# A fused attention and quantized-FFN block on one core: 16-bit split products for q, latent, k and v, new work lists, aligned loops, and q's and k's high halves weighed from PSUM

## The reference, cut to what matters

```python
xn = layernorm(x)
q = xn @ Wq; lat = (xn @ Wk + xn @ Wv) @ W_down_kv          # latent: 64 wide
k, v = lat @ W_up_k, lat @ W_up_v
scores = clip(q_h @ k_h.T / 16) * exp(-1e-4 * |i - j|)      # 16 heads of 16
y = concat(softmax(scores) @ v_h) @ Wo
x1 = x + layernorm(y)
xh = layernorm(x1) @ H
z = quantize_4bit_per_token(xh) @ ternary(weight).T
out = x1 + layernorm(z)
```

## Time and profile before

| | |
|---|---|
| Median of 3 runs | 1436.37 us |
| All runs | 1433.69, 1436.37, 1437.82 us |
| Span of the profiled execution (the page gives no other time of it) | 1433.2 us |
| Granted clock of PE, mean | 0.983 |
| PE, DVE, ACT, POOL busy | 94%, 82%, 77%, 58% |
| Chain that ended last: PE, DVE, issue, ACT, DMA | 76%, 8%, 5%, 4%, 3% |
| Batches in the steady loop | 26 of 32 |

### The profile page before, as it was taken

How to read it: one execution, slowest core, us unless ns; L and a number is a source line. 1 busy time by engine, 2 the same in 40 slices (tenths; PEclk the granted TensorE clock), 3 DMA queues, 4 the chain that set the end, 5 groups by cost and what they waited for, 6 DMA issues and landing times.

```text
span 1433.2 us, 35971 instructions
## 1 busy us (share of the span) xinstructions
PE 1349.5 (94%) x12330; PEld 600.5 (42%) x12330; DVE 1179.9 (82%) x2739; ACT 1098.2 (77%) x1125; POOL 834.7 (58%) x1238
## 2 busy tenths in 40 slices
PE   5889999999999999999999999999999999999863
PEld 3334444444444444444444444444444444443332
DVE  7567888888888888888888888888888888888655
ACT  1878787888888788878878887887888787787831
POOL 4223655666565666556557655656765655675446
PEclk9999999999999999999999999999999999999986
DMA  6455456556555645656564565655556555555420
GB/s 194 154 167 170 154 172 202 155 164 206 164 182 173 197 156 166 206 157 190 173 190 157 173 201 157 193 175 187 156 177 194 163 185 184 176 156 175 128 77 31
DMA packets 174557, 241.45 MB, mean 168 GB/s; under 512 B 28336, under 2 KB 145200, under 8 KB 174512
## 3 DMA queue, kind: packets, MB, share of 16 engines
q1 hardware_dynamic: 140176, 206.78, 46.5%
q10 hardware_dynamic: 34336, 34.08, 7.7%
HBM read 154.80 MB, written 69.21 MB: 156 GB/s over the span
## 4 chain that ended last, share of the span: by engine, by line
PE 76%; DVE 8%; issue 5%; ACT 4%; DMA 3%; SPq 2%; POOL 2%; DVEq 0%; ACTq 0%; POOLq 0%
PE heads_ps L720 27%; PE scores_ps L707 16%; PE misc_ps L603 8%; PE misc_ps L635 7%; PE misc_ps L660 4%; PE misc_ps L614 3%; PE misc_ps L587 3%; ACT probs L909 2%; DVE x_hl L1204 2%; PE misc_ps L595 2%; PE misc_ps L678 2%; DVE diagonal L1253 2%; DVE weighted L1161 2%; PE misc_ps L625 2%; PE misc_ps L669 1%
## 5 line engine op out<-in xcount | busy, mean ns | idle before, releaser
L909 ACT ACTIVATE probs<-scores_ps 128x1024 f32<-128x1024 f32 x768 | 759.8, 1026 | 248.0 <-PE scores_ps L707 247.9
L720 PE MATMUL heads_ps<-probs,v_sb 128*32 128x512 f32 x4096 | 525.4, 603 | 3.6 <-DVE heads L1150 1.9
L1253 DVE TENSOR_TENSOR diagonal<-scores_ps,comp 128x1024 f32<-128x1024 f32 x256 | 312.2, 1219 | 70.1 <-PE scores_ps L707 70.1
L707 PE MATMUL scores_ps<-q_rep,k_rep 64*128 64x128 f16 (+2 forms) x5120 | 324.6, 251 | 16.0 <-DVE diagonal L1253 9.2
L707 PEld LDWEIGHTS scores_ps<-q_rep,k_rep 64*128 64x128 f16 x5120 | 165.6, 94 | 348.7 <-DVE diagonal L1253 149.5
L916 ACT ACTIVATE probs<-diagonal 128x2048 f32<-128x2048 f32 x128 | 246.0, 1922 | 0.0
L996 POOL TENSOR_TENSOR ln_neg_mean<-zero,ln_moments 128x4 f32<-128x4 f32 (+1 forms) x131 | 34.6, 264 | 356.5 <-DVE ln_moments L1115 356.3
L1161 DVE SCALAR_TENSOR_TENSOR weighted<-misc_ps,edges 128x384 f32<-128x384 f32 x256 | 129.4, 547 | 64.3 <-PE misc_ps L603 33.8
L720 PEld LDWEIGHTS heads_ps<-probs,v_sb 128*32 128x32 f32 x4096 | 91.5, 108 | 171.7 <-issue 169.8
L1038 POOL TENSOR_TENSOR q_hl<-weighted,q_hl 128x768 f16<-128x768 f32 x64 | 105.5, 1648 | 77.5 <-DVE q_hl L1168 77.5
L1043 POOL TENSOR_TENSOR heads_c<-heads_c,den_spread 128x1024 f32<-128x1024 f32 (+1 forms) x33 | 75.7, 2296 | 111.0 <-DMA den_spread<-den_scratch 111.0
(11 more groups left out here) (132 smaller groups left out, 1511.5 us busy)
## 6 DMA issues: line engine op xcount, KB each, us to landing
q_rep<-q_scratch SPq DMA_DIRECT2D x128, 384.0 KB, 4.3
k_rep<-k_scratch SPq DMA_DIRECT2D x256, 192.0 KB, 3.9
q_scratch<-q_hl SPq DMA_DIRECT2D x64, 384.0 KB, 2.6
k_scratch<-k_hl SPq DMA_DIRECT2D x64, 384.0 KB, 3.1
x_in<-in_L_attn_x_dram ACTq DMA_DIRECT2D x32, 512.0 KB, 4.9
heads_c<-heads SPq DMA_DIRECT2D x256, 64.0 KB, 2.5
x_res<-in_L_attn_x_dram ACTq DMA_DIRECT2D x32, 512.0 KB, 6.8
den_spread<-den_scratch SPq DMA_DIRECT2D x256, 64.0 KB, 2.3
```

The costliest lines, as they stand in the source:

```text
L707: ins = mm(scores_ps[:, place + par, at:at + n * P], k_rep[rows, pair, kv_, k_cols], q_rep[rows, pair, qv_, q_cols], start=True, stop=True)
L720: ins = mm(heads_ps[W32 * g:W32 * (g + 1), :], v_sb[:, b.slot, kt, at:at + W32], probs[:, quad % 2, g, kt, :], start=(kt == 0), stop=(kt = ...
L909: nc.scalar.activation(flat[:, :, at:at + S], scores_ps[:, place:place + 2, :], ACT.Exp, scale=EXP_SCALE).then_inc(off_probs, 1)
L1253: v.tensor_tensor(diagonal[:, quad % 2, 2 * two:2 * two + 2, :], scores_ps[:, place:place + 2, :], comp[:].rearrange("p t n -> p (t n)").u ...
```

## The change

- **Products.** `w_lat`, `wq`, `w_up_k` and `w_up_v` times 1024 are split once into high and low f16 halves. xT and the latent are split in each batch: ACT casts the high half from PSUM (`x_high_take`, `lat_high_take`), DVE subtracts it from PSUM to get the low half (in place of its copy). Each product becomes three: high by high, high by low, low by high.
- **Weighing.** The f16 high half of q and k comes from a second pair of SCALAR_TENSOR_TENSOR out of PSUM; the cast is gone. The bank is released after that second pair, and POOL's `split` waits for that release.
- **Lists.** All five lists are new, and the closing ones go with them. Entries carry their group, and a heads copy and a pv step can stand in two groups.
- **Loops.** The loop's first instruction is placed at the start of a fetch block (`head_slot`) on each engine.
- The choice of the fast path also tests column sums of squares of the weights; the general path keeps fp32.

```diff
+W_GAIN = 2.0 ** 10
+WEIGHT_BOUND = 32.0
...
 TENSOR_STEPS = {
-    1: [("z", 0, 0), ("z", 1, 0), ("pv_end", 3, 0)], 3: [("xT", 0, 0), ("pv_end", 3, 1)], 5: [("xT", 1, 0), ("pv_end", 3, 2)],
-    7: [("pv_end", 3, 3), ("lat", 0, 0)], 9: [("q", 0, 0), ("q", 0, 1)], 11: [("pv", 0, 0), ("x1T", 0, 0)],
-    13: [("x1T", 1, 0), ("pv", 0, 1)], 15: [("k", 0, 0), ("pv", 0, 2), ("k", 1, 0), ("pv", 0, 3)], 17: [("v", 0, 0), ("xh", 0, 0)],
-    19: [("xh", 1, 0), ("pv", 1, 0)], 21: [("pv", 1, 1), ("pv", 1, 2)], 23: [("q", 1, 0), ("q", 1, 1), ("pv", 1, 3)],
-    25: [("y", 0, 0), ("y", 0, 1)], 27: [("pv", 2, 0), ("qintT", 0, 0)], 29: [("y", 1, 0), ("y", 1, 1)],
-    31: [("pv", 2, 1), ("pv", 2, 2), ("pv", 2, 3)],
+    1: [("xT", 0, 0, "pre"), ("xT", 1, 0, "pre"), ("z", 0, 0, "c")], 3: [("pv", 3, 0, "a")], 5: [("pv", 3, 1, "a")],
+    7: [("pv", 3, 2, "a"), ("pv", 3, 3, "a"), ("z", 1, 0, "c")], 9: [("lat", 0, 0, "pre"), ("q", 0, 0, "pre"), ("q", 0, 1, "pre")],
+    11: [("x1T", 0, 0, "b"), ("pv", 0, 0, "own")], 13: [("k", 0, 0, "pre"), ("pv", 0, 1, "own"), ("x1T", 1, 0, "b")],
+    15: [("k", 1, 0, "pre"), ("pv", 0, 2, "own"), ("pv", 0, 3, "own")], 17: [("v", 0, 0, "pre"), ("xh", 0, 0, "b")],
+    19: [("xh", 1, 0, "b"), ("pv", 1, 0, "own")], 21: [("pv", 1, 1, "own"), ("pv", 1, 2, "own")],
+    23: [("pv", 1, 3, "own"), ("q", 1, 0, "pre"), ("q", 1, 1, "pre")], 25: [("y", 0, 0, "a"), ("y", 0, 1, "a"), ("pv", 2, 0, "own")],
+    27: [("pv", 2, 1, "own"), ("qintT", 0, 0, "b")], 29: [("y", 1, 0, "a"), ("y", 1, 1, "a")], 31: [("pv", 2, 2, "own"), ("pv", 2, 3, "own")],
 }
 SCALAR_STEPS = {
-    4: [("load_res", 0)], 12: [("x1T", 0)], 14: [("x1T", 1)], 15: [("load_x", 0)], 21: [("round_x", 0)],
-    22: [("round_x", 1), ("round_x", 2), ("round_x", 3)], 30: [("qintT", 0)],
+    6: [("xT", 0, "pre"), ("xT", 1, "pre")], 10: [("load_x", 0, "load"), ("lat", 0, "pre")], 11: [("x1T", 0, "b")], 14: [("x1T", 1, "b")],
+    20: [("load_res", 0, "a"), ("round_x", 0, "b")], 23: [("round_x", 1, "b")], 25: [("round_x", 2, "b"), ("round_x", 3, "b")],
+    30: [("qintT", 0, "b")],
 }
 VECTOR_STEPS = {
-    1: [("z", 0), ("z", 1), ("x1_make",)], 2: [("xT", 0)], 5: [("x1_stats",), ("xT", 1), ("x1_moments",), ("z_stats",)],
-    8: [("heads_end", 3)], 10: [("lat", 0), ("q_split", 0), ("z_moments",)],
-    15: [("x1_low", 0), ("x1_low", 1), ("k_split", 0), ("den_invert",), ("k_split", 1)], 17: [("v", 0)],
-    18: [("heads", 0), ("act_scales",)], 20: [("v", 1), ("x_stats",), ("x_moments",), ("q_split", 1)], 25: [("heads", 1)],
-    26: [("quantize",)], 27: [("y", 0)], 28: [("y", 1), ("y_stats",), ("y_moments",), ("heads", 2)],
+    0: [("heads", 2, "a")], 1: [("z", 0, "c"), ("x1_make", "b")],
+    6: [("x1_stats", "b"), ("xT", 0, "pre"), ("xT", 1, "pre"), ("x1_moments", "b"), ("heads", 3, "a")], 7: [("z", 1, "c")],
+    8: [("z_stats", "c")], 10: [("q", 0, "pre"), ("x1_low", 0, "b"), ("lat", 0, "pre"), ("z_moments", "c")], 12: [("k", 0, "pre")],
+    14: [("den_invert", "a"), ("x1_low", 1, "b"), ("k", 1, "pre")], 17: [("v", 0, "pre"), ("heads", 0, "own")],
+    19: [("v", 1, "pre"), ("act_scales", "b")], 21: [("heads", 1, "own")], 25: [("q", 1, "pre"), ("quantize", "b")],
+    26: [("x_stats", "load")], 28: [("x_moments", "load"), ("y", 0, "a"), ("y", 1, "a")], 29: [("y_stats", "a")], 31: [("y_moments", "a")],
 }
-POOL_STEPS = ["x1_apply", ("q", 0), "rstd4", "add_out", ("k", 0), "heads_normalize", ("k", 1), "x_apply", ("q", 1), "rstd2"]
-SYNC_STEPS = [("own", "spread", 1), ("a", "gather_den"), ("a", "pack_den"), ("pre", "store_q", 0), ("a", "compact", 1),
-              ("a", "return_den"), ("a", "spread_den"), ("pre", "store_k", 0), ("pre", "spread", 0), ("own", "compact", 0),
-              ("pre", "store_q", 1), ("pre", "store_k", 1), ("c", "store_out")]
+POOL_STEPS = [
+    ("x1_apply", "b"), ("q", 0, "pre"), ("rstd4", "c"), ("k", 0, "pre"), ("k", 1, "pre"), ("add_out", "c"), ("heads_normalize", "a"),
+    ("q", 1, "pre"), ("x_apply", "load"), ("rstd2", "a"),
+]
+SYNC_STEPS = [
+    ("own", "spread", 1), ("a", "gather_den"), ("a", "compact", 1), ("a", "pack_den"), ("pre", "store_q", 0), ("a", "return_den"),
+    ("pre", "store_k", 0), ("a", "spread_den"), ("pre", "spread", 0), ("pre", "store_k", 1), ("own", "compact", 0), ("pre", "store_q", 1),
+    ("c", "store_out"),
+]
...
+PRODUCTS = ((0, 0), (0, 1), (1, 0))
...
-            with eng.Fori(0, (B - 6) // 2) as loop:
+            with nc.Fori(0, (B - 6) // 2, engines=[eng.engine], head_slot={eng.engine: 0}) as loop:
...
+                    for c in range(DC):
+                        for n, (wh, xh) in enumerate(PRODUCTS):
+                            for half in range(2):
+                                ins = mm(misc_ps[LAT * half:LAT * (half + 1), bank, 0:S // 2], w_lat_hl[:, wh, c, :],
+                                         xT_hl[:, xh, c, half * S // 2:(half + 1) * S // 2], start=(c == 0 and n == 0),
+                                         stop=(c == DC - 1 and n == len(PRODUCTS) - 1))
                 ins.then_inc(in_psum["lat"], 1)
...
+                else:
+                    for n, (wh, xh) in enumerate(PRODUCTS):
+                        ins = mm(misc_ps[:, BANK["q", part], :], wq_hl[:, wh, piece, part * P:(part + 1) * P], xT_hl[:, xh, piece, :],
+                                 start=(piece == 0 and n == 0), stop=(piece == DC - 1 and n == len(PRODUCTS) - 1))
...
+                for n, (wh, lh) in enumerate(PRODUCTS if b.buffers == 2 else PRODUCTS[:1]):
+                    for half in range(2):
+                        rows = slice(LAT * half, LAT * (half + 1))
+                        out_k = misc_ps[:, bank + half, (1 - half) * S // 2:(2 - half) * S // 2]
+                        if b.buffers == 1:
+                            ins = mm(out_k, w_up_k[rows, part * P:(part + 1) * P], latT[rows, :], start=True, stop=True)
+                        else:
+                            ins = mm(out_k, w_up_k_hl[rows, wh, part * P:(part + 1) * P], latT_hl[rows, lh, :],
+                                     start=(n == 0), stop=(n == len(PRODUCTS) - 1))
                 ins.then_inc(in_psum["k"], 1)
...
+            def x_high_take(b, part):
+                act.wait_ge(in_psum["xT"], part_count("xT", b, part))
+                nc.scalar.activation(xT_hl[:, 0, part, :], misc_ps[:, BANK["xT", part], :], ACT.Copy).then_inc(x_high, 1)
+
+            def lat_high_take(b, part):
+                act.wait_ge(in_psum["lat"], part_count("lat", b, 0))
+                nc.scalar.activation(latT_hl[:, 0, :], misc_ps[:, BANK["lat", part], 0:S // 2], ACT.Copy).then_inc(lat_high, 1)
...
-                nc.scalar.dma_start(wq[:], Wq.rearrange("(c p) n -> p c n", p=P)).then_inc(second_loaded, 16)
+                nc.scalar.dma_start(wq, Wq.rearrange("(c p) n -> p c n", p=P)).then_inc(second_loaded, 16)
                 act.wait_ge(second_loaded, 16 * SECOND)
-                nc.scalar.activation(squares[:, 0], wq[:], ACT.Square)
+                nc.scalar.activation(wq_hl[:, 0], wq, ACT.Copy, scale=W_GAIN).then_inc(w_high, 1)
+                for up, up_hl in ((w_up_k, w_up_k_hl), (w_up_v, w_up_v_hl)):
+                    nc.scalar.activation(up_hl[:, 0, :], up, ACT.Copy, scale=W_GAIN).then_inc(w_high, 1)
                 load_x(b.other(1), 0)
+                for part in range(2):
+                    x_high_take(b, part)
+                nc.scalar.activation(squares[:, 0], wq, ACT.Square)
+                lat_high_take(b, 0)
+                act.wait_ge(w_lat_made, 2)
+                nc.scalar.activation(sq_lat, w_lat, ACT.Square, scale=16.0)
...
-                pool.wait_ge(high_done, count(len(SPLITS), b, at + 1))
+                pool.wait_ge(taken[name], part_count(name, b, c))
...
+                dve.wait_ge(x_high, part_count("xT", b, part))
+                v.tensor_tensor(xT_hl[:, 1, part, :], bank, xT_hl[:, 0, part, :], ALU.subtract).then_inc(taken["xT"], 1)
...
+                dve.wait_ge(lat_high, part_count("lat", b, 0))
+                v.tensor_tensor(latT_hl[:, 1, :], bank, latT_hl[:, 0, :], ALU.subtract).then_inc(taken["lat"], 1)
...
+                    else:
+                        ins = v.tensor_scalar(dst, src, 1.0 / W_GAIN ** 2, None, ALU.mult)
...
                 if not (isinstance(b.number, int) and b.number == 0 and at < 2):
                     dve.wait_ge(split_done, count(len(SPLITS), b, at - 1))
                 bank = misc_ps[:, BANK["q", part], :] if name == "q" else k_tokens(part)
-                gain = 16.0 * K_GAIN * (K_GAIN if name == "k" else 1.0)
+                gain = 16.0 * K_GAIN * (K_GAIN / W_GAIN ** 2 if name == "k" else 1.0 / W_GAIN)
+                hl = q_hl if name == "q" else k_hl
                 for ver in range(2):
-                    ins = v.scalar_tensor_tensor(weighted[:, at % 2, ver * EDGE:(ver + 1) * EDGE], bank[:, ver * P:ver * P + EDGE], gain,
```

(11 more changed lines are left out.)

190 lines of the change are left out of this document (115 added, 75 removed), and 9 rows, old and new, of the table TENSOR_CLOSING.

## The result

| | before | changed |
|---|---|---|
| Median | 1437.09 us (4 runs, 1433.69 to 1444.33) | 1556.49 us (4 runs, 1552.14 to 1565.19) |
| Ratio | 1 | 1.0835, 95% interval 1.0804 to 1.0866 |
| Span of the profiled execution | 1433.2 us | 1553.4 us |
| Granted clock of PE, mean | 0.983 | 0.954 |

Times of kernels in this document are medians of fast runs; one execution of d6_plain_loops was slow (2359.0 us), its trace is of that execution, and nothing is read from it.

What follows compares the result with a forecast made beforehand. PE bounds the kernel at 41.84 us a batch; DVE's longer queue leaves nearly all of PE's 2.15 us saving as waits (period 41.75). Span 1433.2 - 2.5 - 3 + 2.5 = 1430.2, so 1433 us; range 1392 to 1460.

Steps and rivals of the forecast that it cites:

- Other terms: Terms beside the period: loops, DMAs and POOL's order at nothing, opening +2.5, first batches -3, steady batches -2.5 or so.
- once a batch 1.02: Price of the weighing's SBUF cast on DVE, to be dropped: 0.56 each, in one case a batch 1.02.
- The walk on DVE: DVE's work in order from first diagonal to k1's weighing end, 20.6 us without waits, setting when PE may start v.
- z's wait of 0.25: DVE waits for z's product, now behind both xT stages: ready at 2.3, asked for at 2.1, +0.25 a batch.
- x_apply (0.45): PE arrives at xT before POOL's x_apply delivers its data, and waits 0.45 a batch.
- my 41.75: Forecast period of a batch: 0.35 + 20.6 + 0.25 + 0.45 + 20.1 us, against 41.84 before.
- the opening: Start of the run: first x, q and latent casts and wq's low half, in an unhidden chain, cost +2.5 us.
- the first three batches: Without z, x1 or x statistics on DVE, they keep more of PE's saving: about -1 each, -3 us.
- stay the bound: Rival: the second pair hides on DVE, PE's whole 2.15 us a batch comes through, 1370 us; chance 22%.
- the second rival: x1_low, ahead of latent on DVE, waits for ACT's cast; period 42.6 if late by one exponential, about 1460; 25%.
- The rival with a q part of 0.79: PE's matmuls run at the skill page's 131 ns spacing, 0.6 us a batch less: 1415 us; chance 2%.
- aligned loops cost or give nothing: Jumps and fetches at the loop turn cost 0 to 2 us in all, so aligning loops was taken as nothing.

Runs made afterwards that it cites:

- d6_plain_loops: Changed kernel with the lists of before, the high half cast from SBUF again, xT's second part early and plain loops: 1508.2 us, ratio 1.0497.
- v1: Changed kernel with one DVE instruction a batch, the square of xscale, moved to POOL: 1465.0 us, ratio 1.0190.
- b1: Kernel before with only POOL's order of the change (both k splits, then add_out, then heads_normalize): 1470.3 us, ratio 1.0235.
- w3: w2 with the high half cast from SBUF again in place of the second weighing pair: 1404.8 us, ratio 0.9777.
- b2: Kernel before with aligned loops alone added: 1437.6 us, ratio 0.9998.
- c2: v1 with plain loops in place of aligned ones: 1543.1 us, ratio 1.0739.
- w2: v1 with add_out between k's two splits and x_apply ahead of q's second split on POOL, x's statistics early on DVE: 1428.1 us, ratio 0.9938.
- d2: d1 with the high half cast from SBUF again and PSUM released after the first pair: 1489.3 us, ratio 1.0363.
- d1: Changed kernel with the lists of before, ACT casts for xT and latent added: 1508.9 us, ratio 1.0487.

## Why the prediction was wrong

**The step that failed** is in "Other terms": "add_out stands before heads_normalize on POOL behind both k splits ... I cost that at nothing: POOL has 15.7 us free a batch". POOL did have the time. I asked whether POOL would be late, and not whom it hinders while it works: its two instructions of 2.4 us now lie over DVE's scale and square, which stand until they end. That is 3.9 us a batch on DVE, ahead of the diagonal on which PE waits, and 1.6 more where the clock falls, in 13 batches of 21. v1 and b1 show it from both sides.

**The trace of before told of it.** A row of mine says it: the cast that took 1.02 in place of 0.56. I wrote "once a batch 1.02" and took it as a price. POOL beside it, in the kernel before:

```profile
773.88 1.67 POOL L1038 TENSOR_TENSOR k_hl<-weighted,k_hl 128x768 f16<-128x768 f32 x1
775.50 0.53 POOL L996 TENSOR_TENSOR ln_neg_mean<-zero,ln_moments 128x4 f32<-128x4 f32 x1
```

The cast was asked for at 774.95, POOL's split ended at 775.55, the cast at 775.97: it waited 0.5. And POOL's next small instruction took 0.53 in place of 0.20, waiting for the cast in its turn. One of the 33 scales took 2345 ns, in the closing part. DVE and POOL there:

```profile
1413.82 2.35 DVE L1217 TENSOR_SCALAR xscale<-absmax 128x2 f32<-128x2 f32 x1
```

```profile
1413.80 2.34 POOL L1056 TENSOR_TENSOR out_sb<-out_sb,x 128x1024 f32<-128x1024 f32 x1
```

This is the meeting itself, with the same POOL instruction, in the trace from which I predicted. In the batch I read, the scale began 0.16 after a POOL instruction ended. The Trainium skill has the rule in "SBUF — State Buffer", section "Who interferes with whom": VectorE and GpSimd share a pair of SBUF ports. A copy, cast or tensor_scalar of VectorE in a two-port mode blocks fully against GpSimd, and so does an instruction with two SBUF inputs against a GpSimd instruction that reads SBUF; the one issued first has the pair to its end. The trace agrees, though it does not show in which mode an instruction ran: the scale (2.08) and the square (2.17) waited, while the weighings, with one input from PSUM, kept 540 to 558 ns over all 512 calls.

**What held.** The walk on DVE from the first diagonal to the end of k1's weighing was 753.31 to 774.23, 20.9 against 20.6 and z's wait of 0.25, with no gap but that wait. A weighing takes 1.86 (1.88), a second pair 0.93 (0.94), a q part 1.40 (1.38); a k stage 0.43 (0.37). PE waited 0.46 for x_apply (0.45), z's product made DVE wait 0.28 (0.25):

```profile
753.85 1.09 PE L604 MATMUL misc_ps<-ident,xn 128*128 128x128 f32 x8 [0.46 <-POOL xn L1086]
```

With the square off DVE the period was 42.9: my 41.75 and the 1.1 that PE waits behind the scale. So the forecast period lacked the meetings and little else. PE's first scores came at 37.05 against 33.72: the opening cost 3.3 (2.5 forecast). A small term failed beside it: the first three batches were to give back 3, and took 1.0 more (PE's scores of the fourth began at 158.45 against 154.15).

**The rivals.** PE did not stay the bound in the changed kernel (86% busy); in w3 it nearly does. x1_low did not hold up the latent batch by batch, as the second rival had it: it waited for ACT 4 times in the run, 4.7 us in all, the longest 3.4:

```profile
DVE x_hl L1292 <- ACT x_hl L918: 4.7, 4, 3.4
```

The rival with a q part of 0.79 is out: a q part takes 1.40. The slower outcome came by a way that I had not named. That aligned loops cost or give nothing was right for before (b2) and wrong as a statement on the changed code, which would lose some 80 us without them (c2 and d6; the changed kernel itself was not run with plain loops).

**Where the 119 us lie.** The square's meeting, with the clock that falls behind it, is 91 (v1). The shorter meeting of the scale and the wait for x_apply are the next 37 together (w2), which ends 9 below the kernel before. The second weighing is 8 to 31, by the order it stands in. Why plain loops stall here and not before stays open.

## What to carry to other kernels

Before an instruction is moved on POOL, look at what DVE does in the same microseconds: an instruction of four columns can stand for as long as POOL's longest. Read the maximum of each small instruction and not only its mean, and explain the odd one before you use it as a price. And when one engine's list is changed, follow each of its steps through the queue that stores its result: the lists of POOL and SP could not be exchanged one by one.

## What the runs showed that I had not expected

- Which instruction meets POOL is decided by tenths of a microsecond: in the kernel before the scale began 0.16 us after a POOL instruction ended; with POOL's order alone changed the scale passed with 0.26 us, and the square 0.1 us behind it stood for 2.33, which made 32 us of the run.
- PE's clock: behind 3.17 us and 2.10 us of standing it was 0.63 and 0.65 over the next 4.6 and 4.9 us in the batches shown, and a q part took 2.5 to 2.7 in place of 1.40. But waits of the same length, in the same place, were followed by a lower clock only in some batches: 13 of 21 in the changed kernel, 16 of 24 in d2, 9 of 24 in d1. What decides it stays open here. Behind 1.08 us (v1) and 1.28 us (b1) it stayed at full speed every time.
- Without alignment two kernels with the new products lost 6 to 7 us a turn of the loop (in the turn read, PE stood still for 4.8 of them), and the one before lost nothing.
